# Steps put in another order in a fused attention and expert kernel: a products-and-eviction pair ahead of a transpose, and the shared layer's products ahead of a block of scores

## What is computed

```python
h = layernorm_affine(concat(cls, patches @ W + b) + pos)      # 37 rows per image
h = concat([h, txt], axis=1)                                  # 37 + 128 = 165 rows of 256
q, k, v = split(layernorm(h) @ W_qkv.T + b_qkv)               # 16 heads of 16
s = (q @ k.T) * 256 ** -0.5                                   # 165 x 165 per head
attn = softmax(where(s is among the 49 largest of its row, s, -inf))
h = h + (attn @ v) @ W_out.T + b_out
x = layernorm(h)
top-8 of 64 experts, 128 slots each, silu(x Wg) * (x Wu) @ Wd, weighted and summed
shared = silu(x Wsg) * (x Wsu) @ Wsd                          # the shared layer
h = h + routed + shared
```

## Time and profile before

| what | value |
|---|---|
| device time, median of 3 runs | 3077.92 us (3074.23 to 3079.49) |
| the profiled execution, its own time | 3077.82 us |
| its span, first to last instruction | 3076.1 us |
| ACT busy over the span | 2480.2 us (81%) |
| DVE busy | 2486.5 us (81%) |
| PE busy | 2360.4 us (77%) |
| POOL busy | 2181.0 us (71%) |
| mean granted TensorE clock | 0.882 |

### The profile page before, as it was taken

The page is one execution under the profiler, slowest core; times in us unless marked ns, Lnnn a source line. Parts: engine busy times, 40 slices in busy tenths (PEclk is TensorE's granted clock), DMA queues, the critical chain, the costliest instruction groups (busy, mean ns, idle before and its releaser), DMA issues.

```text
span 3076.1 us, 74618 instructions
## 1 busy us (share of the span) xinstructions
PE 2360.4 (77%) x17233; PEld 2007.1 (65%) x17233; DVE 2486.5 (81%) x12929; ACT 2480.2 (81%) x11201; POOL 2181.0 (71%) x4319
## 2 busy tenths in 40 slices
PE   5677877778787778777887787787878787764887
PEld 4566666666676666666666676676667676544776
DVE  1798889888888899988989888988899888842444
ACT  3999999999999999989999899998999989811111
POOL 3457777777777777777777777777777777645665
PEclk7799988988999989988899889988888889867998
DMA  2011011010110110101101101001010100006886
GB/s 66 10 30 24 25 27 29 25 30 23 28 25 23 29 30 25 30 23 24 27 25 29 30 25 27 25 22 28 25 30 23 29 18 24 19 16 159 220 222 143
DMA packets 203389, 130.07 MB, mean 42 GB/s; under 512 B 101776, under 2 KB 194444, under 8 KB 202924
## 3 DMA queue, kind: packets, MB, share of 16 engines
q1 hardware_dynamic: 168064, 105.38, 12.7%
q0 software_dynamic: 34368, 19.34, 3.9%
q10 hardware_dynamic: 492, 0.45, 0.1%
HBM read 77.63 MB, written 34.09 MB: 36 GB/s over the span
## 4 chain that ended last, share of the span: by engine, by line
ACT 47%; PE 14%; POOL 13%; issue 11%; DVE 6%; DMA 4%; another core or an unknown queue 2%; ACTq 0%; POOLq 0%; SPq 0%; DVEq 0%
ACT JK L877 23%; ACT E L865 9%; PE bank L1766 4%; ACT PTT L901 4%; DMA out<-E,X 3%; ACT JL L890 3%; POOL slot_token L683 3%; ACT PTI L906 2%; PE bank L1688 2%; PE bank L1691 2%; POOL X L662 2%; POOL out L793 2%; ACT KT L843 1%; PE bank L1757 1%
## 5 line engine op out<-in xcount | busy, mean ns | idle before, releaser
L877 ACT ACTIVATE JK<-S,thr 128x165 f32<-128x165 f32 x2688 | 1120.5, 422 | 14.5 <-POOL thr L624 7.2
L683 POOL DMA_INDIRECT slot_token<-TOKI,SLOT x512 | 533.5, 1042 | 221.8 <-issue 204.4
L662 POOL TENSOR_SCALAR X<-S,nt 128x165 f32<-128x165 f32 x1344 | 582.7, 452 | 75.4 <-DVE LIST L1158 66.1
L865 ACT ACTIVATE E<-bank,nb 128x165 f32<-128x165 f32 x1344 | 508.5, 391 | 10.8 <-DVE S L1083 9.6
L877 ACT ACTIVATION_READ_ACCUMULATOR JK<-S,thr 128x1 f32 x2688 | 510.7, 190 | 0.0
L1277 DVE SCALAR_TENSOR_TENSOR PR<-S,TV,E 128x165 f32<-128x165 f32 x1344 | 480.1, 405 | 0.2
L1083 DVE TENSOR_SCALAR_CACHE_REDUCE S<-bank 128x165 f32<-128x165 f32 x1344 | 364.5, 320 | 86.9 <-PE bank L1691 47.4
L1705 PE MATMUL bank<-IDENT,PR 128*128 128x128 f32 x1344 | 222.2, 283 | 230.3 <-issue 116.1
L1158 DVE MAX8 LIST<-X 128x8 f32<-128x165 f32 x1344 | 351.3, 317 | 8.1 <-DVE X L1148 1.8
L1705 PEld LDWEIGHTS bank<-IDENT,PR 128*128 128x128 f32 x1344 | 154.8, 145 | 284.6 <-issue 163.2
L1688 PE MATMUL bank<-KZ,QA 128*128 128x165 f32 x1408 | 280.8, 346 | 45.6 <-ACT E L865 19.0
(11 more groups left out here) (211 smaller groups left out, 6358.3 us busy)
## 6 DMA issues: line engine op xcount, KB each, us to landing
S<-in_w_gate SPq DMA_DIRECT2D x64, 192.0 KB
S<-in_w_up SPq DMA_DIRECT2D x64, 192.0 KB
E<-in_w_down SPq DMA_DIRECT2D x64, 192.0 KB
RD<-inverses SPq DMA_DIRECT2D x128, 82.5 KB
x_rows<-X SPq DMA_DIRECT2D x64, 160.0 KB
H<-in_txt SPq DMA_DIRECT2D x64, 128.0 KB
QA<-QT SPq DMA_DIRECT2D x512, 10.3 KB
QB<-QT SPq DMA_DIRECT2D x512, 10.3 KB
```

The lines of the kernel that those rows point to most:

```text
L662: last = pool.tensor_scalar(X[n % DEEP][:, t % GROUP, :], S[r % 2][:, t, :], nt[r % 2][:, t:t + 1], DOWN, ALU.add, ALU.mult)
L683: pool.indirect_dma_start(slot_token, bass.IndirectOffsetOnAxis(SLOT[r % 2][:, 0, k:k + 1], 0), TOKI[r % 2][:, :], None, bounds_check=SLOT ...
L865: act.activation(E[r % 2][:, t, :], chunks(bS[g % 3], GROUP, T)[:, t % GROUP, :], ACT.Exp, bias=nb[:, t:t + 1], scale=-1.0, accum_out=sz[: ...
L877: act.activation(JK[:, t % 4, :], S[r % 2][:, t, :], ACT.Sign, bias=(t0, t1)[n][:, t:t + 1], scale=-1.0, accum_out=(c0, c1)[n][:, t:t + 1] ...
```

## The change

On PE the fifth piece of the transposes moves behind `front_v`, and on ACT its copy moves behind the copy of the values. On PE the shared layer's products move ahead of the fourth group of scores. On DVE the two gate steps and the preparation's norm (`front_norm2`) move ahead of the minima of the fourth group (`take(i, r, 3)`). No instruction is added or removed, and SP and POOL keep their streams.

```diff
 ACT
                     exps(i, r, 5)
                     exps(i, r, 6)
-                if has(i - 2):
-                    transposed(i - 2, 4)
                 if has(i + 1):
                     front_v(i + 1, (r + 1) % RING)
                 if has(i - 2):
+                    transposed(i - 2, 4)
                     transposed(i - 2, 5)
 DVE
-                if has(i):
-                    take(i, r, 3)
                 if has(i - 3):
                     back_glu(i - 3)
                     back_glu2(i - 3)
                 if has(i + 1):
                     front_norm2(i + 1, (r + 1) % RING)
                 if has(i):
+                    take(i, r, 3)
                     take(i, r, 4)
 PE
                     back_xt(i - 3, (r - 3) % RING)
+                if has(i - 3):
+                    back_glu(i - 3)
                 if has(i):
                     scores(i, 3)
-                if has(i - 3):
-                    back_glu(i - 3)
-                if has(i):
                     scores(i, 4)
...
                     front_qk(i + 1, 1)
-                if has(i - 2):
-                    transposes(i - 2, 4)
                 if has(i + 1):
                     front_v(i + 1)
                 if has(i - 2):
+                    transposes(i - 2, 4)
                     transposes(i - 2, 5)
                     values(i - 2, (r - 2) % RING)
```

More of the change, by code:

```diff
@@ L1807, in iteration @@
                     back_xt(i - 3, (r - 3) % RING)
-                if has(i):
-                    scores(i, 3)
                 if has(i - 3):
@@ L1812, in iteration @@
                 if has(i):
+                    scores(i, 3)
                     scores(i, 4)
```

## The result

The changed kernel takes 3158.7 us (median of four runs, 3154.3 to 3162.7), the kernel before 3077.6 us on the same chip: ratio 1.026, 95% interval 1.025 to 1.028. It is 81 us slower. The forecast was 65 us slower, 3143 us, with a range of 3085 to 3185 us. The direction, the size and most of the waits that were named came out. Taken by its two steps the forecast did not: step 1 was forecast too dear and step 2 far too cheap, and the two errors partly cancel. The experiments show this.

What follows compares the result with a forecast made beforehand. ACT's work plus 2 to 4 us of waits bounds each round; losses of 0.45, 1.35 and 1.55 us make 3.35 us a set of three, times 19.5 is 65 us: 3143 us, range 3085 to 3185 us.

Steps and rivals of the forecast that it cites:

- step 1: Fifth transposes behind front_v on PE, their copy behind the values' copy on ACT: loss 0.4 or 1.25 us a round.
- step 2: Gate ahead of fourth scores on PE and minima on DVE: PE's chain 0.3 us late, DVE 0.5 us late at most kinds.
- a late word: At VZ: PE's finish is told about 1.2 us after POOL's indirect DMAs end, while they meet SP's query DMAs.
- Step 1, free rounds: Rounds without the long VZ wait, one of every three: reordered copies on ACT take 2.64 us against 2.23, loss 0.4 us.
- Rival C: PE stands longer before the sixth piece and gate, more runs at 1.2 GHz: 3163 us, up to 3185; chance 0.15.
- Step 1, held rounds: Rounds with the long VZ wait, two of every three: front_v's signal stays late, 2.66 us against 1.39, loss 1.25 us.
- rival B: The values escape the late signal and the fifth piece is caught, a loss of 0.4 us there: 3110 us; chance 0.15.
- 19.5 sets: Sets of three rounds, two with the long VZ wait: 84.5 us at 2.19 us each gives 39 such rounds.
- The likeliest case: Values' products still told late, everything else as summed: 65 us slower, 3143 us, its own range 3125 to 3158; chance 0.55.
- VZ's wait longer by 0.5 us a held round: Sign on ACT: VZ's long wait grows by 0.5 us where it occurs, since the fifth copy no longer stands before it.
- A: Nothing is told late, since the fifth piece is pushed behind front_v: faster, 3052 us; chance 0.10.

Runs made afterwards that it cites:

- step 1 alone: Kernel before with only the fifth transposes moved behind front_v on PE and their copy behind the values' copy on ACT: ratio 1.014, 44 us slower.
- step 2 alone: Kernel before with only the gate moved, ahead of the fourth scores on PE and their minima on DVE (both halves): ratio 1.015, 47 us slower.
- DVE's half: Kernel before with only DVE's gate moved ahead of the fourth group's minima, PE's order as before: ratio 1.011, 34 us slower.

## Why the prediction came out as it did

*What bounds the kernel.* Right: a round is ACT's 38 us plus its waits, and DVE is close behind. Of the wait for VZ the prediction said that a late word, bound to POOL's run, holds it. On one chip moving the run away took the wait from 69.3 to 3.2 us, and in step 1 alone a late word 1.3 us behind the run's end met the fifth piece, so the run is very likely part of the cause. What the second chip has otherwise, and how the word is late, stays open.

*Step 1, free rounds.* The term was 0.4 us and measured 1.6. The 0.63 us of the sixth piece's turn is right (0.64 in the row). What the prediction passed over is its own sentence that `front_v` "could start only some 0.1 us earlier": the fifth piece was what PE did in the wait for KT. Without it PE stands 2.26 us, the clock falls, and VZ and the fifth copy wait 0.73 and 0.57 us. Rival C had the falling clock, though it put its price on the sixth piece and the gate, and for step 1 in the held rounds.

*Step 1, held rounds.* The term was 1.25 us and measured 0.6 and 0.4. The step that failed is "so I take it as held". VZ's wait fell by 37 us and the fifth copy's rose by 47, and in 31 of 35 such rounds it is the fifth piece whose word is late: what rival B describes ("a loss of 0.4"). Why 0.1 us and a lower clock were enough to let the products escape isn't shown. In all, 44 us against the 57 that 0.4 + 1.25 + 1.25 makes over 19.5 sets.

*Step 2.* Forecast at 0.3 + 0.1 + 0.3 less 0.25, some 9 us, and measured at 47: the largest error. Three of its sentences failed. "Half-clock time moved to full clock gives some back; I take 0.3": the gate's products took the half clock over, and the chain ended 0.7 us late, 0.5 of it from its start behind X2T and 0.2 more where the sentence took 0.2 back. "In a held round ACT's 0.3 vanish in the wait for VZ": in step 2 alone VZ's wait is 85.2 us against 84.5, so it took up nothing; the release moved with the round. And "DVE loses little": DVE's half by itself costs 34 us, because the minima were work done in a wait. With both halves a wait for the gate's second bank appeared ahead of HT as well (62.4 us, 24.0 before).

*The sum.* Apart the steps measure 44 + 47 = 91 us, together 81; the difference lies within the intervals. The forecast's 57 + 9, some 65, has about the right total of wrong parts; that it came so near is luck. The likeliest case as a whole is not what happened; what did is step 1 by rival B in the held rounds and by the clock in the free ones, and a step 2 that no case had.

*What would show it.* TH's wait nearly gone and one at XT: right, the size low. A wait on the sixth copy: right (48.3 us in all). DVE's wait for `values` longer: right (50.9 to 77.0 in its group). VZ's wait longer by 0.5 us a held round: wrong. The text had said that this would make A or B the case.

## What to carry to other kernels

Before moving work behind a wait, ask what that work was doing where it stood: the minima and the fifth piece were the filling of gaps. Moved behind the gate, the minima cost 34 us, and the gap that the fifth piece left on PE ended in a fall of its clock. When a bound wait stands later in the loop, don't book lateness against it before knowing that its releaser doesn't move too. And a total that comes out proves no term of it: one run for each step is what showed that two of them were wrong. When idle time is filled to raise a clock, read from the trace whether the filling still ends inside the wait: here it pushed the next products back by 0.9 and 2.2 us a round.

## What the runs showed of the hardware

- The granted clock can fall at the very moment that PE resumes: it stood 2.26 us, and in the next 3.44 us the mean granted clock was 0.52. With products of 128 columns put ahead of PE's waits, the mean over the kernel rose from 0.88 to 0.96.
- Raising that clock by such products changed the time by 0.1 to 0.3% here (0.999 and 0.997), although PE's half-clock time fell from 24% of the span to 8% in the first of the two (twice what the mean clock lacks to 1). That is the clock's worth less the delay by the products themselves, `front_v` 2.2 us a round and `back_xt` 0.9 us.
- In two rounds read closely, the word that PE's products are done reached ACT 2.7 and 2.5 us behind their recorded end while POOL issued indirect DMAs, 1.2 and 1.3 us behind the end of that run. It was late for whichever products ended at that time: `front_v` before, the fifth piece in step 1 alone.
- The same kernel took 3030, 3070 and 3085 us on three chips, in medians. On the chip of 3030 us VZ's idle time was under 4 us in each of its four kernels, while in every other trace of a kernel that kept POOL's run of indirect DMAs it added up to 37 to 124 us (of the 124, 111 were for products that fillers put off).
